# A two-layer decoder on one core: gated experts ranked behind the next chunk's attention, a tighter allowance in the last 256 recurrence steps, and values held until the previous bank is turned

## The chip, the cores and the metric

One core of a Trainium2 chip runs the whole decoder as one program. The metric is the device time of one execution in microseconds (us). A change of about 0.2% (3 us) is what a measurement of this kernel can tell from none.

## The reference, cut to what matters

Two layers on `x` of 2 x 1024 x 256 (batch, steps, features), each of the form "x plus f(layernorm(x))", three times:

```
x = x + causal_self_attention(ln(x))          # layer 0, 16 heads of 16
x = x + cross_attention(ln(x), ctx)           # 77 context rows
x = x + linear_experts(ln(x))                 # 8 experts, top 2, no activation
x = x + rnn(ln(x))                            # layer 1: h = tanh(Wi x_t + Wh h + b), 1024 steps in sequence
x = x + cross_attention(ln(x), ctx)           # with biases
x = x + shared_ffn(ln(x)) + gated_experts(ln(x))   # 16 experts of 64, top 4 of 2 groups, silu(g) * u
```

Everything but the recurrence and the keys of the self attention works on each step by itself, so that it can be done in chunks of the sequence as soon as their steps are there.

## The kernel before

The sequence is cut into four chunks of 256 steps (512 columns with both batches). Each part of a layer is a class that registers *kinds* of work with `st.add(engine, name, op, count, cost, rank, ...)`: for example `gat_make` (a matmul of the gated experts' up and gate products, 512 columns), `gat_down` (one of the products back to 256 features), `gat_spread`, `self_scores` and `x_scores` (scores for the exponentials), `self_values` and `x_values` (probabilities times values), `x_first` and `self_first` (the pass that finds the maxima), `x_y` (output product), `lin_make` (layer 0's experts), `back`, `n5_turn`, `n6_turn` (transposes that bring the recurrence's output and the norms into place). The gated experts' work comes in blocks of 128 hidden features: 12 `gat_make`, 4 `gat_down` and, for eight blocks of twelve in a chunk, one `gat_spread`.

`Plan.make` is run when the program is built. It simulates the engines with the costs given and picks, again and again, the kind whose next item could start first; items that could start at the same moment go by rank, the lowest first. Its result is a fixed order for each engine, written into the program. So neither a rank nor an allowance exists on the chip: they only decide which instruction stands behind which.

The recurrence is a chain over 1024 steps. Each step has eight small TensorE products (`hi`, 128 x 2), four more (`lo`), two tanh on ScalarE (L557, L558) and a subtraction on VectorE (L563); the products of both are line L512 in the profile. The planner fills the time between with everything else. Two rules of `Plan.make` bear on that:

- If the next chain item of an engine is due, other work may start only if it would end at most `slack` after the due time. `slack` is `LATE` = 0.3 us, more for work that has been ready for over 6 us.
- Where TensorE would stand idle for over 0.1 us, a *filler* is written into the order (`idle`, L531 in the profile, L535 after): matmuls on a bank that nobody reads, of so many columns as the planned idle time holds. They have no result and keep TensorE going.

A kind can have `opens` (its item takes one of five shared PSUM banks, until the item that `closes` it is done) and `behind` (its item is not placed before another kind has come so far). In the attentions a group of four heads is summed by `values` in a bank named ("self", u) or ("x", u); ScalarE copies it out (`keep`, L642), and `turn_o` (L648) transposes the copy.

Ranks are 1000 c + 3500 for chunk c of layer 1, plus a base: 10 for `n5`, 30 for the cross attention, 40 for `n6`, 50 for the gated experts.

The recurrence needs all of layer 0 for the chunk that it comes to. From step 740 on it is given the input of the last chunk (steps 768 and on), and waits there until layer 0 has it. Behind its last step come `back`, `n5`, the cross attention, `n6` and the gated experts of chunk 3.

The prediction cuts the span at five places: 0 to 229.6 us (the recurrence's first product), to 1016.7 (product of step 740), to 1098.1 (step 767), to 1384.5 (the last), and to the end.

Of the kernel before, what the change touches and what calls it, by code (L numbers as in the profile page):

```python
# [16 lines left out]
P = 128  # L17
B, S, D = 2, 1024, 256
# [16 lines left out]
MH = HID // P  # L35
# [3 lines left out]
class Prog:  # L39
# [6 lines left out]
    def sb(self, name, shape, dt=F32, ctx=None):  # L46
        return (ctx or self.ctx).enter_context(self.nc.sbuf_tensor(self.stage + name, shape, dt))
# [114 lines left out]
SEEN = {"pe": 0.18, "act": 0.10, "v": 0.06, "pool": 0.15, "sp": 2.0}  # L162
PERIOD = 0.79
LATE = 0.3
SECOND = 3500
PATIENCE = 6.0
FULL_CLOCK = 2300
LEAST_GAP = 0.1
# [4 lines left out]
class Plan:  # L173
# [16 lines left out]
    def make(self, programs, trial, signalled):  # L190
# [4 lines left out]
        by_name = {k.name: k for k in self.kinds}  # L195
# [30 lines left out]
        while left:  # L226
            best = None
            for e in SEEN:
                due = expected(e) if guarded else None
                more = max((burst(k) for k in by_engine[e] if k.next < k.count), default=0.0)  # L230
                for k in by_engine[e]:
                    if k.next == k.count:
                        continue
                    if k.ready is None:
                        k.ready = ready_at(k)
                        if k.ready is None:
                            continue
                    at = max(free[e], k.ready)
                    if k.opens and k.opens(k.next) is not None:
                        if not idle:  # L240
                            continue
                        at = max(at, min(idle, key=lambda b: b[0])[0])
                    if any(by_name[name].next < need(k.next) for name, need in k.behind or ()):
                        continue
                    cost = k.cost(k.next)
                    if due is not None and not k.chain and at < due + 0.4:
                        slack = max(self.late + max(0.0, at - k.ready - PATIENCE) * 0.1, more)
                        if at + cost > due + slack:
                            continue
                    key = (at, 0 if k.chain and not burst(k) else 1, k.rank(k.next))  # L250
                    if best is None or key < best[0]:
                        best = (key, k, cost)
# [11 lines left out]
            i, e = k.next, k.engine  # L264
# [5 lines left out]
            if e == "pe":  # L270

                gap = at - free[e] if last_chain and by_name["hi"].next else 0.0
                if gap > LEAST_GAP or burst(k) > LEAST_GAP and by_name["hi"].next:
                    if gap > LEAST_GAP:
                        run[0] = free[e]
                    more = burst(k) if gap <= LEAST_GAP else max(0.0, BURST - gap) * (burst(k) > 0)
# [27 lines left out]
TC = 4  # L304
# [471 lines left out]
class SelfAttention:  # L776
# [6 lines left out]
    def __init__(self, st, w, ln, xT, rank, room):  # L783
# [13 lines left out]
        for j in range(2 * NH):  # L797
            c, i, b, _ = tile_of(j)
            n = 2 * c + i + 1
# [12 lines left out]
        for n, (u, kb) in enumerate(self.blocks):  # L812
# [9 lines left out]
               opens=lambda i: ("self_v", i // KD) if i % KD == 0 else None)  # L822
# [9 lines left out]
               behind=[("self_highest", lambda i: i - FIRST_BANKS + 1)])  # L832
# [9 lines left out]
               behind=[("self_values", lambda i: self.score_items[i][0] - 1)])  # L842
# [1 line left out]
               closes=lambda i: ("self_s", i))  # L844
        st.add("pe", "self_values", self.values, len(self.blocks), 0.7, lambda n: of_block(n) + 0.32,
               opens=lambda n: ("self", self.blocks[n][0] // B) if self.blocks[n][0] % B == 0 and self.blocks[n][1] == 0
               else None)
        self.merge = Merge(st, "self", [(c, w) for c in range(NK)],
                           lambda u: (self.s["pv"], self.block_end[B * u + 1]), rank, room.merge)

# [155 lines left out]
class CrossAttention:  # L1006
# [6 lines left out]
    def __init__(self, st, name, layers, chunks, xT, scr, rank, room, first, later):  # L1013
# [9 lines left out]
        def block(n, m):  # L1023
# [16 lines left out]
               behind=[(name + "_one", lambda i: 1 if i < B else 4)])  # L1040
# [3 lines left out]
               opens=lambda i: (name + "f", i))  # L1044
# [7 lines left out]
               opens=lambda i: (name + "s", i), behind=[(name + "_values", lambda i: i // 2 - 1)])  # L1052
        st.add("act", name + "_exp", self.exp, 2 * len(self.units), 0.52, lambda i: of_unit(i // 2) + 0.31,
               closes=lambda i: (name + "s", i))
        st.add("pe", name + "_values", self.values, len(self.units), 0.7, lambda u: of_unit(u) + 0.32,
               opens=lambda u: (name, u // B) if u % B == 0 else None)
        self.merge = Merge(st, name, [(c, w) for c, w, _ in chunks], lambda u: (s["pv"], B * (u + 1)), rank, room.merge)

    def zero(self, v, layer):
# [603 lines left out]
def all_layers(g, a, out):  # L1663

    with ExitStack() as ctx:
        st = Stage(g, ctx, "", (g.b2, g.b3, g.b4, g.b5, g.b6), LATE)
        nc, sb = g.nc, st.sb
# [9 lines left out]
        self_room, cross_room, gated_room = Weights(), Weights(), Weights()  # L1677
# [31 lines left out]
        w = Weights()  # L1709
# [47 lines left out]
        def rank(layer, base):  # L1757
            return lambda c: when(layer, c) + base

        def tile_rank(layer, base):  # L1760
            return lambda j: when(layer, j // TC) + base

        ln1 = ChunkNorm(st, "n1", lambda i: (g.x_in[i // TC], 32), lambda j: j // TC * AHEAD, xn1,
                        behind=[("qk_make", lambda i: 16 * (i // TC)), ("self_v", lambda i: KD * TC * (i // TC))])
# [5 lines left out]
                        behind=[("xq_make", lambda i: 8 * place[0, i // TC])])  # L1770
# [3 lines left out]
                        behind=[("xq_make", lambda i: 8 * place[1, i // TC])])  # L1774
# [9 lines left out]
        def crossed(layer):  # L1784
            return lambda i: (cross.merge.s["xup"], TC * place[layer, i // TC] + i % TC + 1)
# [6 lines left out]
        rnn = Recurrence(st, rw, ln3, xT3, -5000)  # L1792
        history = AddHistory(st, rnn, tile_rank(1, 0))
        rnn.back, history_in["rnn"] = history.s["turned"], history.s["xup"]
        ln6 = ChunkNorm(st, "n6", crossed(1), tile_rank(1, 40), sb("n6_xn", [P, 1, D]),
                        behind=[("gat_make", lambda i: 12 * MH * (i // TC))])

        gated_room.room_in = (attn.merge.s["y"], 2 * NH)
        gated = GatedExperts(st, w, ln6, rank(1, 50), out, gated_room)

        def load(sp, i):
            if i == 0:
# [160 lines left out]
        def guard_rnn(act):  # L1963
# [8 lines left out]
               behind=[("self_load_k0", lambda i: 1)])  # L1972
# [76 lines left out]
```

## Time and profile before

| | us |
|---|---|
| median of 3 runs (lowest, highest) | 1532.84 (1530.99, 1533.41) |
| profiled execution, own time | 1542.55 |
| its span | 1540.8 |
| TensorE busy | 1492.7 (97%) |
| VectorE busy | 804.9 (52%) |
| ScalarE busy | 591.4 (38%) |
| filler matmuls (L531), busy | 205.3, 829 of them |

The profiled execution took 9.7 us more than the median run. The span leaves out 1.75 us of its own time. A matmul's busy time includes its way through the array, so that busy times of neighbours overlap; how much of TensorE an instruction takes is read from one start to the next.

### The profile page before, as it was taken

How to read it: one execution, taken by the hardware profiler on the slowest of the kernel's cores; microseconds unless marked ns; L12 is line 12 of the kernel's file. 1: busy time of each engine (PE TensorE's matmuls, PEld its weight loads, DVE VectorE, ACT ScalarE, POOL GpSimd, SP SyncE). 2: the span in 40 equal slices, each digit the busy share in tenths (PEclk: the TensorE clock that was granted, in tenths of full speed). 3: DMA queues.
4: the chain of work that ended last, by engine and by line, in shares of the span. 5: the costliest groups of instructions: out<-in, count | busy, mean ns of one | idle time of the engine just before them, and what ended most of it. 6: DMA issues, size and time to landing. Idle time of an engine off the chain costs nothing.

```text
span 1540.8 us, 48664 instructions
## 1 busy us (share of the span) xinstructions
PE 1492.7 (97%) x20001; PEld 1046.0 (68%) x20001; DVE 804.9 (52%) x2574; ACT 591.4 (38%) x2778; POOL 38.3 (2%) x60
## 2 busy tenths in 40 slices
PE   5699989999999999999999999999999999999998
PEld 4465467777777777777777777777676667665555
DVE  5736753277744217977551126855344534553264
ACT  2051305724313773342268764621243224321220
POOL 1000000000000000000000000000000000000000
PEclk9899889999899999999999999999998999999999
DMA  5644000110000002110000005100001000000100
GB/s 153 136 91 101 22 1 3 24 37 3 2 1 3 3 6 37 30 27 2 2 4 3 3 3 160 30 9 2 1 17 37 2 2 16 3 2 28 22 1 14
DMA packets 45470, 40.20 MB, mean 26 GB/s; under 512 B 9723, under 2 KB 44486, under 8 KB 45254
## 3 DMA queue, kind: packets, MB, share of 16 engines
q1 hardware_dynamic: 43526, 36.32, 10.0%
q8 instruction: 162, 2.65, 0.7%
q10 hardware_dynamic: 1728, 0.79, 0.4%
q14 instruction: 54, 0.44, 0.1%
HBM read 25.81 MB, written 10.80 MB: 24 GB/s over the span
## 4 chain that ended last, share of the span: by engine, by line
PE 92%; DVE 3%; DMA 2%; SPq 1%; issue 0%; ACT 0%; DVEq 0%; ACTq 0%
PE b L512 20%; PE b L531 10%; PE b L1591 8%; PE b L1371 8%; PE b L1643 6%; PE b L1000 5%; PE b L971 4%; PE b L737 4%; PE b L916 3%; PE b L693 3%; DVE mx L925 2%; PE b L1252 2%; PE b L1227 2%; PE b L648 2%; PE b L455 1%; PE b L497 1%
## 5 line engine op out<-in xcount | busy, mean ns | idle before, releaser
L512 PEld LDWEIGHTS b<-hp,whp 128*128 128x128 f16 x12276 | 487.3, 96 | 255.8 <-ACT hp L557 139.5
L512 PE MATMUL b<-hp,whp 128*128 128x2 f16 x12276 | 539.4, 166 | 1.7 <-DVE hp L563 0.6
L563 DVE TENSOR_TENSOR hp<-hist,hp 128x4 f16<-128x4 f32 x1023 | 165.1, 161 | 470.3 <-ACT hist L558 462.4
L557 ACT ACTIVATE hp<-b 128x4 f16<-128x4 f32 x1024 | 177.2, 173 | 538.8 <-PE b L512 530.2
L531 PE MATMUL b<-whp 128*128 128x512 f16 (+5 forms) x829 | 205.3, 352 | 0.0
L925 DVE TENSOR_REDUCE mx<-b 128x1 f32<-128x512 f32 (+3 forms) x304 | 189.0, 653 | 1.7 <-PE b L916 1.2
L558 ACT ACTIVATE hist<-b 128x4 f32<-128x4 f32 x1024 | 178.6, 174 | 0.0
L985 ACT ACTIVATE vp<-b 128x512 f32<-128x512 f32 x288 | 171.3, 602 | 18.7 <-PE b L974 11.1
L1591 PE MATMUL b<-vp,heads 128*128 128x512 f16 x576 | 160.7, 382 | 0.0
L1371 PE MATMUL b<-we,xT 128*128 128x256 f32 x512 | 150.3, 410 | 0.0
L916 PE MATMUL b<-heads 128*128 128x512 f16 (+3 forms) x384 | 115.7, 342 | 3.5 <-DVE mx L925 0.4
L1643 PE MATMUL b<-vp,tail 128*128 128x256 f32 x384 | 112.4, 410 | 0.0
L971 PE MATMUL b<-heads 128*128 128x256 f16 (+1 forms) x640 | 100.4, 261 | 0.0
L531 PEld LDWEIGHTS b<-whp 128*128 128x128 f16 x829 | 68.3, 97 | 44.3 <-issue 5.2
L1238 ACT ACTIVATE x_pr<-b 77x512 f32<-77x512 f32 x128 | 72.2, 593 | 61.3 <-PE b L1227 61.0
L1000 PE MATMUL b<-vp 128*32 128x256 f32 (+1 forms) x1280 | 95.3, 370 | 0.2 <-ACT vp L985 0.2
L1371 PEld LDWEIGHTS b<-we,xT 128*128 128x128 f32 x512 | 85.0, 192 | 6.9 <-issue 1.0
L1395 DVE SCALAR_TENSOR_TENSOR x<-b,wts,x 128x256 f32<-128x256 f32 x128 | 61.8, 483 | 43.5 <-PE b L1371 39.2
L1643 PEld LDWEIGHTS b<-vp,tail 128*128 128x128 f32 x384 | 64.7, 192 | 10.3 <-issue 5.4
L441 POOL TENSOR_TENSOR rs<-ve,neg_half 128x2 f32<-128x2 f32 x48 | 34.1, 710 | 1435.8 <-DVE ve L435 1435.8
L1591 PEld LDWEIGHTS b<-vp,heads 128*128 128x128 f16 x576 | 47.9, 97 | 26.5 <-issue 0.3
L1197 DVE TENSOR_REDUCE x_nm<-b 128x4 f32<-128x308 f32 x128 | 54.6, 468 | 18.8 <-PE b L1188 18.7
(203 smaller groups left out, 1568.5 us busy)
## 6 DMA issues: line engine op xcount, KB each, us to landing
x_qs<-qx_scr SPq DMA_DIRECT2D x48, 128.0 KB
qx_scr<-xq_pair SPq DMA_DIRECT2D x16, 256.0 KB, 2.1
heads<-q_scr SPq DMA_DIRECT2D x24, 128.0 KB, 4.5
heads<-k_scr SPq DMA_DIRECT2D x36, 64.0 KB, 2.7
x<-in_x SPq DMA_DIRECT2D x8, 256.0 KB, 6.8
q_scr<-tail SPq DMA_DIRECT2D x8, 256.0 KB, 2.3
k_scr<-tail SPq DMA_DIRECT2D x8, 256.0 KB, 2.5
we<-in_L_ffn_We SPq DMA_DIRECT2D x2, 1024.0 KB
```

Source lines behind the costliest of these rows:

```text
L512: return pe.matmul(self.z(t)[:, m], self.w.whp[:, a, k, m * P:(m + 1) * P], self.g.hp16[:, (t - 1) % 2, part, k, :], start=False, stop=Tru ...
L531: pe.matmul(self.g.b7[:, 0:min(512, columns - at)], self.w.whp[:, 0, 0, 0:P], self.w.whp[:].rearrange("p a k n -> p (a k n)")[:, 0:min(512 ...
L557: act.activation(self.g.hp16[:, t % 2, 0], self.z(t), ACT.Tanh, scale=1 / LIFT).then_inc(self.s["hi_ready"], 1)
L558: act.activation(self.g.hist[:, :, :, t % (4 * HALF)], self.z(t), ACT.Tanh, scale=1 / LIFT).then_inc(self.s["full_ready"], 1)
L563: v.tensor_tensor(self.g.hp16[:, t % 2, 1], self.g.hist[:, :, :, t % (4 * HALF)], self.g.hp16[:, t % 2, 0], ALU.subtract).then_inc(self.s[ ...
L925: v.tensor_reduce(self.mx[:, column(j) // P, head:head + heads, int(first > 0)], self.st.bank("self_first", i)[:, 0:P * n * heads].rearran ...
L971: last = pe.matmul(o[:, N * e:N * e + N], self.ks[:, b, h // 2, P * kb:P * kb + P], self.qs[:, h, QW * b + first:QW * b + QW], start=True, ...
L985: act.activation(self.pr[:, n % 2, e0:e0 + heads, first:QW], self.st.bank("self_s", i)[:, 0:N * heads].rearrange("p (e n) -> p e n", e=hea ...
L1000: last = pe.matmul(o[QD * e:QD * e + QD, QW * b + first:QW * b + QW], self.va[:, b * (S // P) + kb, at:at + QD], self.pr[:, n % 2, e, firs ...
L1371: last = pe.matmul(o[:, D * (e % 2):D * (e % 2) + D], self.xT[:, k, column(j):column(j) + P], self.w.we[:, k, D * e:D * e + D], start=k == ...
L1591: last = pe.matmul(o[:], wt[:, k, m * P:(m + 1) * P], x[:, k, :], start=at == 0, stop=at == 5)
L1643: last = pe.matmul(o[:, D * (p % 2):D * (p % 2) + D], self.hT[:, n % 3, P * p:P * p + P], self.w.wd[:, m, :], start=m == 0 and p % 2 == 0, ...
```

## The change

Three edits, all of them to what the planner is told. No instruction of the computation is added or removed; only their order, the banks and the fillers differ.

- The norm `n6` and the gated experts of layer 1 get 1200 more rank, so that those of chunk c come behind the attention of chunk c+1 instead of ahead of it. `n6_turn` of a tile also waits for `gat_xl` of the tile before.
- Once 768 tanh have been placed, other work may end at most 0.06 us behind the chain's due time instead of 0.3.
- The first `values` of a new bank is not placed before `turn_o` of the group before it.

```diff
+HURRY = 768
+HURRIED = 0.06
 SECOND = 3500
+BEHIND = 1200
...
                     if due is not None and not k.chain and at < due + 0.4:
-                        slack = max(self.late + max(0.0, at - k.ready - PATIENCE) * 0.1, more)
+                        late = self.late if by_name["tanh"].next < HURRY else HURRIED
+                        slack = max(late + max(0.0, at - k.ready - PATIENCE) * 0.1, more)
...
         st.add("pe", "self_values", self.values, len(self.blocks), 0.7, lambda n: of_block(n) + 0.32,
                opens=lambda n: ("self", self.blocks[n][0] // B) if self.blocks[n][0] % B == 0 and self.blocks[n][1] == 0
-               else None)
+               else None, behind=[("self_turn_o", lambda n: self.blocks[n][0] // B - 1)])
...
         st.add("pe", name + "_values", self.values, len(self.units), 0.7, lambda u: of_unit(u) + 0.32,
-               opens=lambda u: (name, u // B) if u % B == 0 else None)
+               opens=lambda u: (name, u // B) if u % B == 0 else None,
+               behind=[(name + "_turn_o", lambda u: u // B - 1)])
...
-        ln6 = ChunkNorm(st, "n6", crossed(1), tile_rank(1, 40), sb("n6_xn", [P, 1, D]),
-                        behind=[("gat_make", lambda i: 12 * MH * (i // TC))])
+        ln6 = ChunkNorm(st, "n6", crossed(1), tile_rank(1, 40 + BEHIND), sb("n6_xn", [P, 1, D]),
+                        behind=[("gat_make", lambda i: 12 * MH * (i // TC)), ("gat_xl", lambda i: i - 1)])
...
-        gated = GatedExperts(st, w, ln6, rank(1, 50), out, gated_room)
+        gated = GatedExperts(st, w, ln6, rank(1, 50 + BEHIND), out, gated_room)
```

**Behind the last step (TensorE).** The place is the stretch just after the recurrence's last product. Before (L1643 is `gat_down`, L595 `back`, L455 a norm's turn, L737 `xq_make`, L1188 `x_first`, L531 filler):

```order
L1643 MATMUL b<-vp,tail 128x256 x12
L595 MATMUL b<-ident,hist 128x128 x4
L531 MATMUL b<-whp 128x512 x23
L531 MATMUL b<-whp 128x256
L455 MATMUL b<-ident,n_xn 128x128 x2
L531 MATMUL b<-whp 128x512 x3
L531 MATMUL b<-whp 128x128
L455 MATMUL b<-ident,n_xn 128x128 x2
L737 MATMUL b<-xT,first 128x256 x8
L531 MATMUL b<-whp 128x512 x91
L531 MATMUL b<-whp 128x192
L1188 MATMUL b<-first,x_qs 128x154 x12
```

The same place after the change, where every line number is up to 5 higher (L1596 is `gat_make`, L1625 `gat_spread`, L1648 `gat_down`):

```order
L599 MATMUL b<-ident,hist 128x128 x4
L1648 MATMUL b<-vp,tail 128x256
L1625 MATMUL b<-mp,sel_pair 128x512
L1648 MATMUL b<-vp,tail 128x256
L1596 MATMUL b<-vp,heads 128x512 x12
L1625 MATMUL b<-mp,sel_pair 128x512
L1648 MATMUL b<-vp,tail 128x256 x2
L459 MATMUL b<-ident,n_xn 128x128 x2
L1648 MATMUL b<-vp,tail 128x256 x2
L1596 MATMUL b<-vp,heads 128x512 x3
L459 MATMUL b<-ident,n_xn 128x128 x2
L741 MATMUL b<-xT,first 128x256 x8
```

Chunk 2's gated blocks, which before all stand ahead of `back`, now stand in the places of the fillers between `back`, the norm, the projection and the first pass.

**At step 740 (TensorE).** The place is the stretch where the recurrence waits for layer 0's last chunk (L63 with `wg` is that chunk's gate product, L1371 is `lin_make`, L1379 `lin_bias`, L1591 `gat_make`). Before:

```order
L1591 MATMUL b<-vp,heads 128x512 x4
L1643 MATMUL b<-vp,tail 128x256 x8
L455 MATMUL b<-ident,n_xn 128x128 x2
L63 MATMUL b<-wg,xT 128x8 x4
L1643 MATMUL b<-vp,tail 128x256 x4
L63 MATMUL b<-wg,xT 128x8 x4
L1591 MATMUL b<-vp,heads 128x512 x33
L1356 MATMUL b<-ident,wts 8x128 x4
L1591 MATMUL b<-vp,heads 128x512 x2
L1371 MATMUL b<-we,xT 128x256 x16
L1379 MATMUL b<-be,wtsT 128x256
```

After (L1376 is `lin_make`, L1384 `lin_bias`, L516 the recurrence's products, L535 filler):

```order
L1376 MATMUL b<-we,xT 128x256
L516 MATMUL b<-hp,whp 128x2 x8
L1376 MATMUL b<-we,xT 128x256 x11
L1384 MATMUL b<-be,wtsT 128x256
L1596 MATMUL b<-vp,heads 128x512
L535 MATMUL b<-whp 128x512 x2
L535 MATMUL b<-whp 128x384
L1376 MATMUL b<-we,xT 128x256 x16
L1384 MATMUL b<-be,wtsT 128x256
L1376 MATMUL b<-we,xT 128x256 x9
```

The gated experts' 39 `gat_make` and 12 `gat_down` that stood in the wait are gone from it but for one, and the recurrence goes on until `lin_make` has begun.

**In the last 256 steps (TensorE).** The place is the turning of the sums of chunk 2's cross attention in layer 1 (L648 is `turn_o`, L673 the turn behind it). Before:

```order
L512 MATMUL b<-hp,whp 128x2 x8
L648 MATMUL b<-ident,x_osb 128x128 x4
L512 MATMUL b<-hp,whp 128x2 x4
L531 MATMUL b<-whp 128x512 x7
L531 MATMUL b<-whp 128x320
L512 MATMUL b<-hp,whp 128x2 x12
L648 MATMUL b<-ident,x_osb 128x128 x4
L512 MATMUL b<-hp,whp 128x2 x12
L531 MATMUL b<-whp 128x512 x2
L531 MATMUL b<-whp 128x448
```

After (L652 is `turn_o`, L677 the turn behind it):

```order
L516 MATMUL b<-hp,whp 128x2 x8
L652 MATMUL b<-ident,x_osb 128x128 x4
L516 MATMUL b<-hp,whp 128x2 x4
L1648 MATMUL b<-vp,tail 128x256
L535 MATMUL b<-whp 128x512 x5
L535 MATMUL b<-whp 128x320
L516 MATMUL b<-hp,whp 128x2 x12
L677 MATMUL b<-ident,x_on 128x128 x2
L1648 MATMUL b<-vp,tail 128x256
L516 MATMUL b<-hp,whp 128x2 x12
```

Here too `gat_down` of the chunk before stands where fillers stood.

## Rows read from the trace of the kernel before

**Rows 1.** The page, part 1: busy time of each engine.

```profile
PE 1492.7 (97%) x20001; PEld 1046.0 (68%) x20001; DVE 804.9 (52%) x2574; ACT 591.4 (38%) x2778; POOL 38.3 (2%) x60
```

**Rows 2.** The page, part 4: the chain that ended last, by engine.

```profile
PE 92%; DVE 3%; DMA 2%; SPq 1%; issue 0%; ACT 0%; DVEq 0%; ACTq 0%
```

**Rows 3.** Busy time by stage: stretch, length, engines, granted clock, DMA share, GB/s.

```profile
0.00:229.60 229.60, 187.98 (x1166) 127.96 (x1167) 140.18 (x336) 57.13 (x122) 13.72 (x25) 0.92 0.37 84
229.60:1016.70 787.10, 786.20 (x13183) 576.34 (x13182) 417.11 (x1478) 393.85 (x1932) 16.77 (x24) 0.99 0.08 19
1016.70:1098.10 81.40, 81.40 (x661) 59.51 (x661) 40.72 (x112) 13.22 (x71) 1.37 (x2) 0.94 0.01 1
1098.10:1384.50 286.40, 285.46 (x4181) 195.91 (x4179) 140.02 (x503) 101.35 (x601) 4.29 (x6) 0.98 0.04 11
1384.50:1540.80 156.30, 151.63 (x817) 86.31 (x816) 66.83 (x147) 25.80 (x53) 2.17 (x3) 1.00 0.07 16
```

**Rows 4.** The same stages, fillers (L531) alone: TensorE, weight loads, clock, DMA.

```profile
229.60:1016.70 787.10, 115.99 (x452) 35.32 (x452) 0.99 0.08 19
1016.70:1098.10 81.40, 3.25 (x13) 1.20 (x13) 0.94 0.01 1
1098.10:1384.50 286.40, 40.70 (x160) 12.16 (x158) 0.98 0.04 11
1384.50:1540.80 156.30, 45.32 (x206) 19.66 (x206) 1.00 0.07 16
```

**Rows 5.** The same stages, tanh (L557) alone: one for each step.

```profile
229.60:1016.70 787.10, 128.02 (x739) 0.99 0.08 19
1016.70:1098.10 81.40, 4.84 (x28) 0.94 0.01 1
1098.10:1384.50 286.40, 44.03 (x255) 0.98 0.04 11
```

**Rows 6.** TensorE in order of time, tail: start, us, line, operation, shape, count.

```profile
1407.66 2.54 PE L1643 MATMUL b<-vp,tail 128*128 128x256 f32 x11
1410.04 0.60 PE L595 MATMUL b<-ident,hist 128*128 128x128 f32 x4
1410.48 5.24 PE L531 MATMUL b<-whp 128*128 128x512 f16 x24
...
1420.30 19.89 PE L531 MATMUL b<-whp 128*128 128x512 f16 x92
1440.03 1.18 PE L1188 MATMUL b<-first,x_qs 128*128 128x154 f16 x12
```

**Rows 7.** Busy time in five gated blocks of chunk 3, columns as in group 3.

```profile
1506.70:1530.90 24.20, 24.20 (x107) 13.54 (x106) 10.36 (x16) 2.98 (x5) 0.00 (x0) 1.00 0.00 1
```

**Rows 8.** TensorE in order of time: two steps of the recurrence.

```profile
1136.54 0.52 PE L512 MATMUL b<-hp,whp 128*128 128x2 f16 x12
1136.91 0.54 PE L531 MATMUL b<-whp 128*128 128x512 f16 x2
1137.32 0.52 PE L512 MATMUL b<-hp,whp 128*128 128x2 f16 x12
```

**Rows 9.** The same, a step with a `values` item.

```profile
1302.66 0.48 PE L512 MATMUL b<-hp,whp 128*128 128x2 f16 x12
1303.07 0.64 PE L1252 MATMUL b<-x_pr,first 77*32 77x256 f32 x8
1303.64 0.45 PE L512 MATMUL b<-hp,whp 128*128 128x2 f16 x12
```

**Rows 10.** The wait at step 740: `gat_make` (L1591), then `gat_down` (L1643), alone.

```profile
1016.70:1061.10 44.40, 10.26 (x44) 4.13 (x43) 1.00 0.00 1
1016.70:1061.10 44.40, 5.59 (x24) 4.49 (x24) 1.00 0.00 1
```

**Rows 11.** A stretch at the lower clock, columns as in group 3.

```profile
1174.50:1184.70 10.20, 10.20 (x87) 6.34 (x85) 4.51 (x17) 1.77 (x12) 0.69 (x1) 0.50 0.00 0
```

**Rows 12.** TensorE in order of time, the output product before and in that stretch.

```profile
1169.96 1.11 PE L693 MATMUL b<-first,x_onT 128*128 128x256 f32 x4
1170.90 0.24 PE L512 MATMUL b<-hp,whp 128*128 128x2 f16 x4
...
1174.43 1.19 PE L693 MATMUL b<-first,x_onT 128*128 128x256 f32 x2
1175.41 0.40 PE L512 MATMUL b<-hp,whp 128*128 128x2 f16 x8
```

**Rows 13.** The copies behind the sums (L642): ns min/median/max.

```profile
L642 ACT ACTIVATE tail<-b x16: 597/597/618, 91.2 to 917.6; 128x512 f32<-128x512 f32 x16
```

## The prediction

> **What bounds the kernel now.** I read the engines' shares first: TensorE is busy 97% of the span, VectorE 52%, ScalarE 38% [rows 1], and the chain that ended last runs over TensorE for 92% [rows 2]. By stage, TensorE is busy 188 of the 229.6 us before the recurrence starts, and practically all the time from there on [rows 3]. But busy does not mean useful: 829 of its matmuls are fillers [rows 4]. So I count the span from the first step on as useful work plus fillers, and the question is how many filler columns the new order needs. What a filler costs: the 92 in the tail's longest stretch are 46,784 columns (91 x 512 + 192 in the order), and the next instruction starts 1440.03 - 1420.30 = 19.73 us behind their first [rows 6], so 2371 columns in a us. Adding up all filler rows of the order before gives 362,112 columns, 153 us.
>
> How a step of the recurrence takes up other work: with a filler alone between two sets of 12 products, the sets start 1137.32 - 1136.54 = 0.78 us apart [rows 8]. With one `values` item, which itself takes 1303.64 - 1303.07 = 0.57, they are 0.98 apart [rows 9], that is 0.57 + 0.41. So a step costs what stands in it plus about 0.4, but never less than about 0.78: below 0.4 us of content nothing is saved. The 1022 steps between the first and the last product took 1154.9 us (three stages of [rows 3], 739 + 28 + 255 tanh in [rows 5]), 1.13 each, so most steps are content-bound, and there work moved out of them shortens them.
>
> The tail shows where an engine only kills time. At the last step TensorE still has 25 us of chunk 2's gated work ahead of it (1384.5 to 1410.0), then `back`; and only then starts the chain of chunk 3's attention, with 24 places of fillers in it, together 98,560 columns or 41.6 us, waiting for the norm, the trip of the queries through DRAM and the maxima [rows 6].
>
> **The change part by part.** Useful work is the same in both programs, so the sum has three terms: fillers, steps too light to gain, and new waits.
>
> Fillers. The order after has 265,792 columns in 619 matmuls: 96,320 fewer, at 2371 in a us 40.6 us. They go like this: before step 740 +5,120 columns (+2.2 us), from 740 to 767 -1,472 (-0.6), in the last 256 steps -20,288 (-8.6), in the tail -79,680 (-33.6).
>
> What moves between the stages, from counting the kinds in both orders:
> - *Start.* 14 `self_scores` and 6 `self_values` of chunk 1 stand ahead of the first step now. With 0.57 for a `values` [rows 9] and about 0.22 for a score that is 6.5 us. VectorE is busy only 140 of 229.6 us here and TensorE waits for 42 [rows 3], so part may be hidden: between 0 and +6.5. I take the full 6.5, since what is not paid here is work that the recurrence is rid of either way (next item), and keep the other end for the range.
> - *Steps 0 to 740.* Work +6.4 (16 `x_first`, 8 `gat_down`, 5 `lin_make` come in, the scores and values above go out), fillers +2.2, light steps -1.4: +7.2.
> - *Steps 740 to 767.* Before, the wait holds 44 `gat_make` and 12 `gat_down`, 10.26 and 5.59 us [rows 10], 0.233 and 0.466 each. In these 27 steps the change has 45 `gat_make`, 18 `gat_down` and 5 `gat_spread` less: 10.5 + 8.4 + 1.5 = 20.4, with the smaller exchanges and fillers 21.8 less. The cover of layer 0's last gates (which gated work hid before) is now the recurrence itself: its products stand ahead of `lin_make` and between its first items in the order. If that cover failed, the wait for the gates and their ranking, some 12 us, would be bare.
> - *Steps 767 to 1022.* Work -6.3, fillers -8.6. But steps with under 0.45 us of content go from 20 to 58 of 255 there, and in the whole recurrence from 204 to 236 of 1022; each is held up by the 0.78 floor. With the measured surplus of each content class that is +3.3 here, +2 in all. Together -11.6.
> - *Tail.* Exactly three gated blocks of chunk 2 are left over for it, 36 `gat_make`, 12 `gat_down` and 3 `gat_spread`. Five blocks take 24.20 us [rows 7], so three are +14.5; fillers -33.6: -19.1. The 57 `gat_make`, 17 `gat_down` and 5 `gat_spread` between `xq_make` and the first `x_first` are some 21 to 23 us where fillers held 19.7: the chain is delayed there by 1 to 3, which is part of the sum.
>
> Waits. TensorE's order is fixed, so a `turn_o` that now stands ahead of `values` holds those up until ScalarE's copy is done, 0.6 us [rows 13]. The copy has one to three other items' time to hide behind (a score, 0.22 to 0.45 us, in the start; a step of the recurrence, 0.8, elsewhere). I take +0.5 in all; the bounds are 0 and, for 48 of them wholly bare at 0.6 + 0.2, 38.
>
> Sum: 6.5 + 7.2 - 21.8 - 11.6 - 19.1 = -38.8, with the waits -38. (By the totals: -40.6 + 2 + 0.5, the same.) Span 1540.8 - 38 = 1502.8; the profiled execution's own time 1542.55 - 38 = 1504.5. It was 9.7 above the median of its runs, so the median is forecast at 1532.84 - 38 = 1494.8, say 1495.
>
> The clock. The granted clock is 1.00 but for a few stretches: from the stage means the time at the lower level (1.2 GHz) in the recurrence is 2 x (0.01 x 787.1 + 0.06 x 81.4 + 0.02 x 286.4) = 37 us [rows 3]. Before one of these falls TensorE had no gap, only narrow products: the pairs of the output product start every 0.47 us at full clock ((1170.90 - 1169.96) / 2) and take 0.98 at 0.50 [rows 11, 12]. I leave this term at zero: after the change there are both fewer fillers and more wide gated products among such narrow ones. Bounds: none of it left would give back half of 37, -18; twice as much would cost as much again, +18. Neither has anything in the order for its full size, so I keep -10 to +18.
> The Trainium skill (TensorE: Matmul & The Clock Gate, "HAM oscillation — how this bites in real kernels") advises against idle gaps and prices a slow stretch at half its length. The trace agrees on the price (0.98 for 0.47) but not on idleness as the only cause. By that rule, taking fillers away is safe only as long as other work takes their place, which the order shows in the tail.
>
> **The rivals.**
> - *A. The sum holds, -38.* Chance 0.66. Own range -28 to -47.
> - *B. The attention chain is stretched, and real waits take the fillers' place: about -20.* For it: VectorE and ScalarE serve their queues in order, and chunk 2's gated work (10.36 us of VectorE for five blocks [rows 7], 2.1 a block, 0.7 an instruction) now stands ahead of the tail norm's and the queries' small steps. Five hand-overs at one to three such instructions are 3.5 to 10 us in the tail; the same in the two chunks before is as much again. Against it: VectorE is busy only 67 of 156 us there [rows 3]. Chance 0.17, -27 to -8.
> - *C. The start hides the extra work, and low-clock stretches disappear: -50.* TensorE's 42 us of gaps in the start speak for it; that VectorE does the same reductions before the first experts speaks against. Chance 0.08.
> - *D. The clock: -20.* If narrow attention work gets less company (more steps under 0.45 us of content in the last 256), the 37 us of low clock in the recurrence may double, half of it a loss: +18, so -20 in all. Chance 0.03.
> - *E. Slower: +3 and up.* The one mechanism is the `turn_o` ahead of `values`: 16 groups of the self attention and 32 of the cross attention, 48. If the copy with its signals is bare each time, 0.6 + 0.2 us, it costs 38 and eats all; from 0.85 us each the kernel is slower. Against it: in the recurrence another step stands between nearly always. Chance 0.03.
> - *F. No change within 0.2%:* parts of B, D and E together, 0.03.
>
> **How the numbers follow.** A's -38 gives 1495. Two in ten are left out if the range reaches from -50 to -19: 1483 to 1514. Faster by over 0.2% (about 3 us, what a measurement of this kernel can tell from no change): A, B, C and D, 0.94. Same 0.03, slower 0.03.
>
> **What the profile after would show.** Fillers 619, some 112 us of columns; first step's product 3 to 7 us later than 229.6; product 740 at 1024 to 1034; product 767 at 1084 to 1094; the last at 1360 to 1370; tail 134 to 142 us, with one gated product or other right behind `xq_make` and no gap over 1 us before `x_first`. The forecast is wrong if TensorE shows gaps over 1 us in the tail or bare waits of L512 behind L652 (B, E), if the clock is at 0.5 for much more than 40 us in the recurrence (D), or if TensorE's work ahead of step 0 costs nothing (C).

## The result and the profile after

The changed kernel runs in 1494.26 us, the median of 4 runs (1487.59 to 1500.45), against 1532.68 before: ratio 0.975, 95% interval 0.9704 to 0.9796. That is 38.4 us less by the medians, 31 to 45 by the interval; the forecast was 1495. The profiled execution took 1496.71, with a span of 1494.9.

First the page after, part 1, then its chain by engine. Against [rows 1] and [rows 2] hardly anything differs: the same bound, less of it.

```profile
PE 1450.1 (97%) x19791; PEld 1020.8 (68%) x19791; DVE 807.8 (54%) x2574; ACT 593.3 (40%) x2778; POOL 37.8 (3%) x60
...
PE 93%; DVE 4%; SPq 1%; DMA 1%; issue 0%; ACT 0%; DVEq 0%; ACTq 0%
```

The 210 matmuls that are missing are fillers, 619 for 829. Busy time by the same five stages, columns as in [rows 3]:

```profile
0.00:227.40 227.40, 188.20 (x1262) 126.28 (x1263) 141.61 (x336) 63.74 (x136) 13.62 (x25) 0.94 0.37 85
227.40:1018.80 791.40, 791.00 (x13186) 580.84 (x13185) 429.29 (x1513) 389.38 (x1925) 16.52 (x24) 0.99 0.09 19
1018.80:1077.10 58.30, 58.30 (x585) 44.46 (x584) 28.16 (x83) 14.99 (x73) 1.37 (x2) 0.97 0.01 2
1077.10:1357.60 280.50, 279.86 (x4048) 190.95 (x4046) 135.18 (x488) 97.17 (x589) 4.12 (x6) 0.93 0.05 11
1357.60:1494.90 137.30, 132.75 (x716) 78.29 (x715) 73.54 (x157) 28.01 (x57) 2.17 (x3) 1.00 0.08 18
```

The fillers alone in four of them, which answer to [rows 4]:

```profile
227.40:1018.80 791.40, 118.90 (x459) 36.68 (x459) 0.99 0.09 19
1018.80:1077.10 58.30, 1.95 (x9) 0.88 (x9) 0.97 0.01 2
1077.10:1357.60 280.50, 32.85 (x111) 9.18 (x109) 0.93 0.05 11
1357.60:1494.90 137.30, 9.97 (x42) 3.87 (x42) 1.00 0.08 18
```

| stage | before, us | after | difference | forecast |
|---|---|---|---|---|
| start | 229.6 | 227.4 | -2.2 | +6.5 |
| steps 0 to 740 | 787.1 | 791.4 | +4.3 | +7.2 |
| steps 740 to 767 | 81.4 | 58.3 | -23.1 | -21.8 |
| steps 767 to 1022 | 286.4 | 280.5 | -5.9 | -11.6 |
| tail | 156.3 | 137.3 | -19.0 | -19.1 |
| span | 1540.8 | 1494.9 | -45.9 | -38 |

The two profiled executions differ by more than the medians, since that of before was a long one (9.9 us over this median, that of the change 2.5 over its own). How far single stages can be trusted shows in a second pair of profiles: the two kernels with the bare tail, further down, have the same orders up to the last step. Between those the start is 5.0 us longer after the change (230.8 for 225.8), steps 0 to 740 are 13.1 longer (796.4 for 783.3), steps 740 to 767 are 23.0 shorter and the last 256 are 6.9 shorter. Of the 13.1 some 8 are the clock (27 us at the lower level for 7, at the price found below). So the table's first two rows carry several us of chance, and the third and fourth hold. The tail of before came again at 156.3 us, in the kernel with the hold alone.

The tail, TensorE in order of time (start, us, line, operation, shape, count). Where [rows 6] has 25 us of gated work ahead of `back` (L595 there, L599 here) and 92 fillers behind the projection, `back` now starts 1.5 us behind the last product, and gated blocks stand between the projection (L741) and the first pass (L1193):

```profile
1358.64 0.59 PE L1648 MATMUL b<-vp,tail 128*128 128x256 f32 x2
1359.08 0.60 PE L599 MATMUL b<-ident,hist 128*128 128x128 f32 x4
...
1366.81 3.62 PE L741 MATMUL b<-xT,first 128*128 128x256 f32 x16
1370.27 2.11 PE L1596 MATMUL b<-vp,heads 128*128 128x512 f16 x9
1372.31 0.39 PE L1625 MATMUL b<-mp,sel_pair 48*128 48x512 f16 x1
1372.62 1.99 PE L1648 MATMUL b<-vp,tail 128*128 128x256 f32 x8
...
1391.96 0.70 PE L1648 MATMUL b<-vp,tail 128*128 128x256 f32 x2
1392.49 0.30 PE L1193 MATMUL b<-first,x_qs 128*128 128x154 f16 x2
```

From `back` to the first pass it is 33.4 us now and was 30.0 (1410.04 to 1440.03): the chain itself is 3.4 us longer, the tail 19.0 shorter, because nothing stands ahead of the chain any more.

The stage of the last 256 steps gained 5.7 us less than forecast. It holds a stretch of 27.3 us at 1.2 GHz that the kernel before does not have; columns as above:

```profile
1296.50:1323.80 27.30, 27.30 (x291) 18.04 (x292) 11.26 (x45) 6.15 (x42) 1.41 (x3) 0.50 0.07 21
```

### The profile page after: what moved, and what is told of

The parts are those of the page before. It is cut to its first block, busy times and chain, and to the rows that moved or that the text cites. A ratio compares the mean times of both kernels' runs of the same rounds, so it can differ in the third digit from the quotient of the medians.

```text
span 1494.9 us, 48244 instructions
## 1 busy us (share of the span) xinstructions
PE 1450.1 (97%) x19791; PEld 1020.8 (68%) x19791; DVE 807.8 (54%) x2574; ACT 593.3 (40%) x2778; POOL 37.8 (3%) x60
## 4 chain that ended last, share of the span: by engine, by line
PE 93%; DVE 4%; SPq 1%; DMA 1%; issue 0%; ACT 0%; DVEq 0%; ACTq 0%
PE b L516 21%; PE b L1596 9%; PE b L1376 9%; PE b L535 8%; PE b L1648 7%; PE b L1004 6%; PE b L975 5%; PE b L741 4%; PE b L920 3%; PE b L697 3%; DVE mx L929 3%; PE b L1257 2%; PE b L1232 2%; PE b L459 2%; PE b L652 2%; PE b L501 1%
## 5 line engine op out<-in xcount | busy, mean ns | idle before, releaser
L516 PEld LDWEIGHTS b<-hp,whp 128*128 128x128 f16 x12276 | 486.7, 96 | 257.9 <-ACT hp L561 138.7
L516 PE MATMUL b<-hp,whp 128*128 128x2 f16 x12276 | 536.6, 165 | 0.9 <-ACT hp L561 0.2
L1596 PE MATMUL b<-vp,heads 128*128 128x512 f16 x576 | 166.0, 386 | 0.0
L535 PE MATMUL b<-whp 128*128 128x512 f16 (+6 forms) x619 | 163.7, 353 | 0.0
L1376 PE MATMUL b<-we,xT 128*128 128x256 f32 x512 | 148.8, 406 | 0.0
L1648 PE MATMUL b<-vp,tail 128*128 128x256 f32 x384 | 118.7, 418 | 0.0
L920 PE MATMUL b<-heads 128*128 128x512 f16 (+3 forms) x384 | 112.0, 333 | 5.2 <-DVE mx L929 2.0
L1376 PEld LDWEIGHTS b<-we,xT 128*128 128x128 f32 x512 | 83.1, 189 | 5.6 <-issue 1.0
L1648 PEld LDWEIGHTS b<-vp,tail 128*128 128x128 f32 x384 | 64.0, 195 | 7.7 <-issue 4.1
L535 PEld LDWEIGHTS b<-whp 128*128 128x128 f16 x619 | 50.6, 98 | 26.2 <-issue 4.4
L1596 PEld LDWEIGHTS b<-vp,heads 128*128 128x128 f16 x576 | 48.4, 97 | 25.3 <-issue 0.3
L975 PEld LDWEIGHTS b<-heads 128*128 128x128 f16 x640 | 54.7, 96 | 10.6 <-issue 3.4
```

The lines of the kernel that those rows point to most:

```text
L516: return pe.matmul(self.z(t)[:, m], self.w.whp[:, a, k, m * P:(m + 1) * P], self.g.hp16[:, (t - 1) % 2, part, k, :], start=False, stop=Tru ...
L535: pe.matmul(self.g.b7[:, 0:min(512, columns - at)], self.w.whp[:, 0, 0, 0:P], self.w.whp[:].rearrange("p a k n -> p (a k n)")[:, 0:min(512 ...
L975: last = pe.matmul(o[:, N * e:N * e + N], self.ks[:, b, h // 2, P * kb:P * kb + P], self.qs[:, h, QW * b + first:QW * b + QW], start=True, ...
L1376: last = pe.matmul(o[:, D * (e % 2):D * (e % 2) + D], self.xT[:, k, column(j):column(j) + P], self.w.we[:, k, D * e:D * e + D], start=k == ...
L1596: last = pe.matmul(o[:], wt[:, k, m * P:(m + 1) * P], x[:, k, :], start=at == 0, stop=at == 5)
L1648: last = pe.matmul(o[:, D * (p % 2):D * (p % 2) + D], self.hT[:, n % 3, P * p:P * p + P], self.w.wd[:, m, :], start=m == 0 and p % 2 == 0, ...
```

## The experiments

Theory 1 is the prediction's: time is TensorE's useful work plus filler columns at 2371 in a us, with a floor of 0.78 us for a step. It gives each kernel a time from its order alone. The rivals stand in the expectations. All ratios are to the kernel before, on the same chip. In the diffs `HURRIED = LATE` takes the tight allowance away and `BEHIND = 0`, with the added condition of `n6_turn` taken off, the new rank. Those two parts of the rank edit were not tried apart from each other.

### One edit at a time

The rank alone: the changed kernel with these lines as they were or switched off.

```diff
-HURRIED = 0.06
+HURRIED = LATE
...
-               else None, behind=[("self_turn_o", lambda n: self.blocks[n][0] // B - 1)])
+               else None)
...
-               behind=[(name + "_turn_o", lambda u: u // B - 1)])
```

Expected: 

> The kernel before with the new rank alone. Theory 1 (time is useful TensorE work plus filler columns at 2371 in a us, with a floor of about 0.78 us for a light step): the order has 305,920 filler columns against 362,112, so -23.6 us in the ratio's terms 0.985, of it about -23 in the tail, where 54,144 filler columns are left of 98,560. Theory 2 (the rank is the whole change, the other two edits are small additions): as fast as the full change, 0.975. Rival 3 (gated work ahead of the tail norm stretches the attention chain): 0.99 or more.

Measured: 1508.11 us, 0.984 (0.9807 to 0.9873), or -24.5 us against -23.6 of theory 1. The tail took 133.2 us, 23.1 less than before (23 forecast). Theory 2's 0.975 is excluded, and so is rival 3's 0.99 with a stretched chain.

The allowance alone:

```diff
-BEHIND = 1200
+BEHIND = 0
...
-               else None, behind=[("self_turn_o", lambda n: self.blocks[n][0] // B - 1)])
+               else None)
...
-               behind=[(name + "_turn_o", lambda u: u // B - 1)])
```

Expected: 

> The kernel before with the tighter allowance in the last 256 steps alone. Theory 1: the last 256 steps get 29 us shorter, and the tail 26 us longer, because the same gated work then stands behind the last step: -3 us, 0.998, with 338,752 filler columns of which 50,304 are in the tail. Rival 2 (shorter steps are the gain): about -12 or more, 0.99. In both the stage of steps 767 to 1022 should be well under 286 us.

Measured: 1523.46, 0.9926 (0.9903 to 0.9949), 11 us less. The last 256 steps and the tail by themselves:

```profile
1091.00:1340.20 249.20, 248.87 (x3978) 172.12 (x3975) 110.09 (x424) 91.97 (x576) 2.76 (x4) 1.00 0.05 12
1340.20:1522.00 181.80, 176.63 (x983) 103.19 (x982) 98.73 (x225) 38.52 (x79) 3.65 (x5) 0.99 0.06 14
```

The steps are 37 us shorter than before and the tail 25.5 longer (26 forecast): the gated work was only pushed behind the last step. The forecast missed 8 us of the first number. Of them some 5 may be the clock, 1.00 here for 0.98 in [rows 3]; the rest is not explained. The interval excludes both forecasts of the total, 0.998 and 0.99. The rival's figure came out nearer, but not its reason: the steps give 37 and the tail takes two thirds back.

Holding values alone:

```diff
-HURRIED = 0.06
+HURRIED = LATE
...
-BEHIND = 1200
+BEHIND = 0
```

Expected: 

> The kernel before with the values held behind turn_o alone. Theory 1: 359,040 filler columns, 1.3 us less; the moved work at the start is either paid (sum -2.3 us, 0.998) or hidden in the start's gaps (sum -9 us, 0.994); the first product of the recurrence tells: at 236 us if paid, at 227 to 230 if hidden. Rival (waits for ScalarE's copy are bare, 0.8 us at each of 48): +38 us, 1.025, with gaps ahead of L652.

Measured: 1528.01, 0.9948 (0.9921 to 0.9975), 8 us less, which excludes the 2.3 of work that is paid in full. The first product came at 232.0 us in this profile, between the two places forecast (236, and 227 to 230), so this one profile does not decide between them; twelve together do, below. The rival of bare waits is refuted: TensorE's idle time ahead of `turn_o` is 2.2 us in the whole profile, here and in the changed kernel, and 2.1 in that before. Those of this kernel and of the change (L652; microseconds, times) are the same:

```profile
  issue: 1.6, 4
  ACT x_pr L1243: 0.3, 1
  ACT x_osb L646: 0.3, 1
```

### One edit left out

Without the tight allowance:

```diff
-HURRIED = 0.06
+HURRIED = LATE
```

Expected: 

> The changed kernel with the allowance back at 0.3 us throughout. Theory 1: 306,560 filler columns, 64,576 in the tail; the last 256 steps 19 us longer and the tail 5 us shorter than in the change, so 14 us slower than it: -24.5 against before, or -31 if the start's extra work is hidden: ratio 0.980 to 0.984. Rival 2 (edits add, and the allowance alone is worth 3 us): -35, 0.977.

Measured: 1508.07, 0.9832 (0.9804 to 0.986); -25.8 us, between theory 1's two figures. The last 256 steps took 291.0 us and the tail 132.8. So beside the new rank the allowance is worth some 13 us. Alone it is worth 11, but in another place: there it gains in the steps and pays in the tail, here the gated work that it pushes behind the last step falls into the attention chain's filler places (138 fillers in the tail without it, 42 with it).

Without the hold:

```diff
-               else None, behind=[("self_turn_o", lambda n: self.blocks[n][0] // B - 1)])
+               else None)
...
-               behind=[(name + "_turn_o", lambda u: u // B - 1)])
```

Expected: 

> The changed kernel with the values free of turn_o, as before. Theory 1: 272,192 filler columns, 6,400 more than the change, start and other stages together 35 us under before against 39 to 45 for the change: 0.977 to 0.978, or 2 to 10 us slower than the change; the step-740 stage is 16 us longer and the stretch before it 8 us shorter than in the change. Rival (the start's extra work is paid, and holding values costs waits): as fast as the change or up to 4 us faster, with the first product at 227 to 230 us.

Measured: 1502.16 (1491.86 to 1506.93), 0.9811 (0.9765 to 0.9857). The interval overlaps that of the change, so the total is inconclusive; at -29 us it is 6 short of the -35 that theory 1 gives. In the stages the one at 740 took 72.6 us, 14.3 longer than in the change (16 forecast), the stretch before it 781.6, 9.8 shorter (8 forecast). The first product came at 225.3, not at the rival's 227 to 230.

Without the rank:

```diff
-BEHIND = 1200
+BEHIND = 0
...
-                        behind=[("gat_make", lambda i: 12 * MH * (i // TC)), ("gat_xl", lambda i: i - 1)])
+                        behind=[("gat_make", lambda i: 12 * MH * (i // TC))])
```

Expected: 

> The changed kernel with the gated experts' old rank, so the other two edits alone. Theory 1: 341,376 filler columns; the stage at 740 15 us shorter, the last 256 steps 27 us shorter and the tail 24 us longer than before; the start hidden: -10 us, 0.9935, with a further 5 us where the last 256 steps keep the clock as they did with the allowance alone. Rival (the allowance carries the change): under 0.985.

Measured: 1524.45, 0.9937 (0.9911 to 0.9964). The stage at 740 took 63.2 us, 18.2 less than before (15 forecast), the last 256 steps 264.3, 22.1 less (27 forecast), the tail 179.5, 23.2 more (24 forecast). The allowance does not carry the change. The last 256 steps, columns as before:

```profile
1082.10:1346.40 264.30, 263.98 (x3998) 180.49 (x3996) 111.52 (x427) 93.64 (x579) 2.77 (x4) 0.93 0.05 11
```

With the allowance alone that stage took 249.2 us at a clock of 1.00, with nearly the same filler columns (92,480 there, 89,280 here). The difference of 15.1 us goes with 37 us at the lower clock.

### The tail without fillers

```diff
-                    self.order[e].append(("idle", int((max(gap, 0.0) + more) * FULL_CLOCK // 64) * 64))
+                    if by_name["hi"].next < by_name["hi"].count:
+                        self.order[e].append(("idle", int((max(gap, 0.0) + more) * FULL_CLOCK // 64) * 64))
```

In the kernel before. Expected: 

> The kernel before without the 206 fillers behind the recurrence's last step (they have no result). Theory 1a (the fillers stand for real waits of the attention chain): TensorE is bare for about the same 41 us, the tail stays at 150 to 157 us if the clock holds, and grows by up to 20 us where it falls to half. Rival 1b (the fillers are longer than the waits, so that the queries' trip through DRAM ends well before the 19.7 us filler does): the tail is up to 15 us shorter, 0.99. The gaps ahead of L1189, L1206 and L1228 tell how long each wait really is.

Measured: 1532.4, 1.0002 (0.9976 to 1.0028). TensorE in order of time, with its idle time and what ended it in brackets:

```profile
1403.15 0.60 PE L596 MATMUL b<-ident,hist 128*128 128x128 f32 x4
1408.07 0.41 PE L456 MATMUL b<-ident,n_xn 128*128 128x128 f32 x2 [4.32 <-DVE n_xn L449]
1409.15 0.66 PE L456 MATMUL b<-ident,n_xn 128*128 128x128 f32 x2 [0.67 <-DVE n_xn L449]
1409.60 4.86 PE L738 MATMUL b<-xT,first 128*128 128x256 f32 x16
1425.85 5.15 PE L1189 MATMUL b<-first,x_qs 128*128 128x154 f16 x32 [11.38 <-issue]
1432.70 1.01 PE L1206 MATMUL b<-ident,x_nm 128*16 128x128 f32 x4 [1.71 <-DVE x_nm L1198]
1437.22 1.90 PE L1228 MATMUL b<-x_qs,first 128*77 128x256 f16 x8 [3.50 <-DMA x_qs<-x_mp]
```

The whole tail by engine:

```profile
1377.60:1531.60 154.00, 122.74 (x611) 71.76 (x610) 67.05 (x147) 26.13 (x53) 2.18 (x3) 0.88 0.07 16
```

Both theories hold in part. The wait for the queries is 11.4 us bare, and the filler over it took 19.7: there the filler was longer than the wait. From `back` to the first pass it is 22.7 us here, for 30.0 with fillers and 33.4 with gated work. But the granted clock of the tail fell from 1.00 to 0.88, and the products that follow ran at half speed (the first pass 5.15 us), so that the tail as a whole took 154.0 instead of 156.3. So a part of the fillers stood for real waits: 21.6 us in the five brackets above, 27.1 in the whole tail, where the fillers held 41.6. Gated work that stands in those waits takes no time of its own; what is beyond them lengthens the chain, but it is work that had to be done anyway.

In the changed kernel. Expected: 

> The changed kernel without the 42 fillers behind the last step, 18,880 columns, 8 us. Theory 1a: same time as the change within 3 us, 0.975, with short gaps in the fillers' places. Rival 1b: up to 6 us faster than the change, since every step of the chain starts when its input is there. If the clock falls for want of work, up to 5 us slower.

Measured: 1494.39, 0.9749 (0.9695 to 0.9803), the same ratio as the change; at 8 us to either side it cannot tell theory 1a from a rival of 6 us. The profiled execution was the longest of the four (1507.74). Its tail took 140.1 us for 137.3, with 6.8 us of gaps and 10.2 at the lower clock.

### No filler at all

```diff
-        for at in range(0, columns, 512):
+        for at in range(0, 0, 512):
```

Expected: 

> The changed kernel with no filler matmul anywhere. Theory 1 (in the recurrence fillers stand in waits of the chain and hold the clock): without them the low-clock time, some 60 us in the change, grows clearly and the kernel is slower than the change, 0.98 to 1.02. Rival (fillers cost their own time: a step is content plus 0.4, so a filler longer than the true wait delays it): faster than the change by some of the 104 us of filler columns that the recurrence holds, 0.93 to 0.97.

Measured: 1526.45, 0.994 (0.9902 to 0.9977): some 30 us slower than the change. The rival's 0.93 to 0.97 is excluded. The stages:

```profile
228.00:1053.80 825.80, 797.53 (x12728) 592.82 (x12727) 430.25 (x1512) 389.30 (x1925) 16.66 (x24) 0.86 0.08 18
1053.80:1109.30 55.50, 55.29 (x576) 42.86 (x575) 27.27 (x82) 14.30 (x73) 1.37 (x2) 1.00 0.01 2
1109.30:1384.90 275.60, 266.94 (x3939) 184.87 (x3939) 136.06 (x490) 97.05 (x590) 4.12 (x6) 0.89 0.05 11
1384.90:1524.50 139.60, 128.67 (x674) 75.52 (x673) 73.77 (x156) 27.98 (x56) 2.17 (x3) 0.96 0.08 18
```

TensorE sees far more of the lower clock (0.86 over steps 0 to 740, for 0.99), and these steps take 34.4 us more. In the last 256 steps even 0.89 costs nothing against the change (275.6 for 280.5). So the rival may have some truth: where fillers stand in waits that are shorter than planned they cost, and only what they save in the clock makes them pay. No run takes the two apart.

Nor are all fillers planned waits, as the rule given for them above has it. Ahead of every 32nd step the planner lengthens the filler until TensorE's planned run without a break is 1.7 us (`BURST_STEPS = 32`, `BURST = 1.7` in the kernel), and starts the step that much later. Before the change 31 fillers stand at such places in the recurrence with 86,272 columns, after it 31 with 87,936, which is 37 us at 2371 in a us and a third of all filler columns. They are nearly the same in both orders and so drop out of the difference. But a part of their time is spent on purpose and not in a wait, and this run takes them out with the others.

This limits theory 1. It prices an order as the planner writes it, with its fillers; it does not say that a filler taken out is its time gained.

### The allowance where it hurts

```diff
-HURRY = 768
+HURRY = 512
```

Expected: 

> The changed kernel with the tight allowance from step 512 instead of 768. Theory 1: the recurrence runs ahead to step 740 and waits there for layer 0: the order has 454,336 filler columns, 188,544 more than the change, of which 74,624 stand at step 740. The stretch before is 30 us shorter than in the change, the one from 740 to 767 some 118 us longer, the whole 42 to 48 us slower than the kernel before: ratio 1.027 to 1.031. Rival (letting the recurrence go first is good wherever it is done, the chain is the bound): 0.97 or less.

Measured: 1574.31, 1.0268 (1.023 to 1.0305), 41 us slower than before, where 42 to 48 were forecast. Steps 740 to 767, by engine and then the fillers alone:

```profile
1000.00:1178.20 178.20, 176.48 (x1478) 113.69 (x1478) 93.78 (x249) 68.48 (x180) 4.23 (x6) 1.00 0.16 43
...
1000.00:1178.20 178.20, 38.01 (x168) 15.72 (x167) 1.00 0.16 43
```

178.2 us for 58.3 in the change: 120 more, 118 forecast. The recurrence reaches step 740 only 19 us earlier (the steps before it took 771.1 us, 20 less than in the change, 30 forecast; 37 us of them at the lower clock, 14 in the change) and waits there for layer 0's last chunk, whose work had been held back. Hurrying the chain gained only where all that it will wait for is done; from step 768 on that is so.

### Shorter planned landings

```diff
-        st.add("sp", name + "_load_max", self.load_max, N, 1.3, lambda n: rank(n) + 0.25, after=3.5)
+        st.add("sp", name + "_load_max", self.load_max, N, 1.3, lambda n: rank(n) + 0.25, after=2.0)
```

Expected: 

> The changed kernel, planned with 2 us for 3.5 for the landing of the cross attention's maxima alone. Theory 1: 253,504 filler columns and the start as before: 3 to 5 us faster than the change, 0.972. Rival: bare waits ahead of L1232, 0.975 or more.

Measured: 1479.11 (1476.81 to 1484.66), 0.9638 (0.9607 to 0.9668): faster than both kernels, and 15 us faster than the change. Its last two stages:

```profile
1072.50:1337.60 265.10, 264.44 (x4044) 183.11 (x4042) 134.08 (x488) 97.14 (x588) 4.13 (x6) 1.00 0.05 11
1337.60:1475.10 137.50, 132.83 (x718) 78.15 (x717) 74.18 (x157) 28.81 (x57) 2.17 (x3) 1.00 0.06 18
```

Only 5 us were forecast, from 12,288 fewer filler columns. The rest is in the last 256 steps: 265.1 us at a clock of 1.00, where the change has 280.5 at 0.93, with nearly the same filler columns (47,808 and 47,296). The rival's bare waits did not come: TensorE stood idle ahead of L1232 for 7.6 us in all, and for 8.0 in the change.

With the queries' landing planned shorter too:

```diff
-        st.add("sp", name + "_load_q", self.load_q, N, 5.0, lambda n: rank(n) + 0.21, after=8.0)
+        st.add("sp", name + "_load_q", self.load_q, N, 5.0, lambda n: rank(n) + 0.21, after=5.0)
```

Expected: 

> The changed kernel, planned with shorter landing times for the cross attention's queries (5 us behind their issue for 8) and maxima (2 for 3.5), near the bare waits of 11.4 and 3.5 us that the tail without fillers showed. No wait on the chip is changed, only the order. Theory 1: 252,928 filler columns, 12,864 fewer than the change: 3 to 5 us faster than it, 0.972. Rival (data lands later than planned under load, so bare waits appear and the clock falls): 0.975 to 0.98 with gaps ahead of L1193 or L1232.

Measured: 1492.47, 0.9723 (0.9697 to 0.9748), the forecast's 0.972; its interval overlaps that of the change, so the gain over it is not shown. Its last 256 steps took 275.4 us with 20.5 at the lower clock. Why that clock time is there in the one and not in the other is open: the two orders differ in many places.

## Why the prediction was right, step by step

- **Conserved work plus fillers: held.** The order's 40.6 us less of fillers, 2 for light steps and 0.5 for waits gave -38; the medians differ by 38.4. The same count put four other orders in place: -23.6 forecast and -24.5 measured for the rank alone, -24.5 to -31 and -25.8 without the tight allowance, -10 and -9.7 without the rank, +42 to +48 and +41 with the allowance from step 512 on. It missed by 8 us with the allowance alone, by 6 without the hold (-35 and -29, in a wide interval), and by 11 in the best kernel. That last miss is nearly all the clock: the mean of the four runs is 0.985 there and 0.974 in the change, 32 us less of the lower level, or 12 us of time at the price found below.
- **The tail: right to 0.1 us** (-19.1, -19.0). The three blocks left over and the lost fillers are what the trace shows, and the delay between the projection and the first pass, forecast at 1 to 3 us, was 2.5 (25.7 us for 23.2).
- **Steps 740 to 767: right** (-21.8, -23.1); no bare wait took the place of the gated work (TensorE is busy for all of the 58.3 us), with the recurrence's products as the cover.
- **The start: mis-sized.** +6.5 was taken from bounds of 0 and 6.5. The start is the same order in all seven profiled kernels with the hold and with the planned landings as they were: there the first product comes at 227.4 to 232.0, mean 229.9. In the five without the hold it comes at 225.3 to 229.6, mean 227.1. So the 6.5 us of added work cost 2.8. The prediction's and rival C's reason for less was that TensorE's 42 us of gaps hide the work. But in the same profiles the gaps are 40.6 us in the mean with the hold and 41.6 without, which hides 1 us. What else differs is the time at the lower clock, 27 us for 40. It may account for the rest, but why the order with the hold has less of it is not shown. The early start is also why the first product (forecast at 3 to 7 us behind 229.6) and the products of steps 740 (1024 to 1034), 767 (1084 to 1094) and the last (1360 to 1370) came before their forecast ranges, at 227.4, 1018.8, 1077.1 and 1357.6.
- **The last 256 steps: the clock was mis-sized.** It was taken at zero, within bounds of -10 and +18. From the stage's 0.93, 2 x 0.07 x 280.5 = 39 us are at the lower clock, for 2 x 0.02 x 286.4 = 11 before. Against the kernel with 1.00 there, 39 us of it go with 15.4 us of time, 0.39 each; the pair without the rank and with the allowance alone gives 15.1 for 37, 0.41. The change's own runs say the same: 1500.45 us at a mean clock of 0.969 and 1487.59 at 0.980, that is 93 and 59 us of lower clock, 12.9 us for 34, 0.38 each. So do the runs of the kernel before: a straight line through the times and clocks of the 16, 19 and 15 that stand beside the experiments has a slope of 0.35, 0.39 and 0.40. So 28 us more of it cost some 11. Without that the stage would have gained 17 instead of 6, more than the 11.6 forecast; those 5 us the other way are not explained.
- **Rival D, the clock, came in part.** In the recurrence 2 x (0.01 x 791.4 + 0.03 x 58.3 + 0.07 x 280.5) = 59 us are at the lower clock, for 37 before, against the sign of much more than 40 that the prediction names. Its mechanism, that lighter steps bring the clock down, is not shown: an order with nearly the same filler columns in that stage kept 1.00. The price is under the half that the Trainium skill names (TensorE: Matmul & The Clock Gate, "HAM oscillation — how this bites in real kernels"). A light step shows how a price under the half comes about. With two fillers of 512 columns in it, it takes 0.78 us in [rows 8] and 1.06 inside the 27.3 us stretch, not twice as long, which is 0.26 us for each us at the lower clock:

```profile
1308.89 0.51 PE L516 MATMUL b<-hp,whp 128*128 128x2 f16 x12
1309.25 0.91 PE L535 MATMUL b<-whp 128*128 128x512 f16 x2
1309.95 0.51 PE L516 MATMUL b<-hp,whp 128*128 128x2 f16 x12
```

- **Waits behind `turn_o`: right.** 0.1 us more of gaps there, 0.5 taken, 38 feared in rival E.
- The start's miss (3.7 us too much, by the twelve profiles) and the unexplained 5 us of the last 256 steps have the opposite sign of the clock's (11 us too little), and they nearly cancel. The interval of the measurement reaches from 31 to 45 us. That the total came out to half a us is luck; that it came out within some 10 us is the count of fillers and moved work.
- **B, the stretched chain:** 3.4 us of stretch from `back` to the first pass, none of it lost, as work stands in it.

## What to carry to other kernels

When one engine is full and its order is fixed, count what the order makes it do besides useful work. Here the difference of two orders in that count gave the difference in time to within 2 us in most cases, although no busy share moved. It was off by 6 to 11 us in three, and in two of these the clock accounts for most of it. Keep independent work for the latency chain at the end instead of finishing it before the chain starts: work ahead of the chain is paid in full, work inside it only as far as it is longer than the chain's waits (27 us bare in this tail). And letting a critical chain hurry paid here only where what it depends on later is not the work that is held back for it (13 us gained from step 768 on; from 512 on, some 80 lost against the change).

## What was not expected of the hardware

The same program's runs spread by 13 us (1487.59 to 1500.45) with its granted clock (0.980 to 0.969), at 0.38 us of time for each us at 1.2 GHz. The level falls without any gap on TensorE: ahead of the 27.3 us stretch stood 8.4 us of narrow products (256 columns at most, and the recurrence's of two), in which TensorE was busy for all 8.4, and inside it TensorE was busy throughout. An order of nearly the same content (the one with the shorter landing of the maxima) had none of it in that stage. Fillers hold the clock through the recurrence (0.99 with them, 0.86 without, over steps 0 to 740), but whether the planned ones do it or the one at every 32nd step was not tried, and neither more nor fewer of them explains that one stretch, which came again at the same place in the kernel with the bare tail. What starts and what ends it stays open.
